# Attention denominators spread by a VectorE shuffle, per-slot restacking and a new order of work in two six-layer transformer stacks

## The reference

```python
def _L2_xcond_ref(x, noise_emb, context, src_mask, ctx_mask, ...):      # _L3_xcond_ref is the same
    NL, D, H, DFF = (6, 128, 16, 512); HD = D // H
    def _adaln(x, emb, w, b):
        g, be = jnp.split(emb[:, 0, :] @ w.T + b, 2, axis=-1)
        return _ln(x) * (1.0 + g[:, None, :]) + be[:, None, :]
    def _attn(q, k, v, mask):
        scores = jnp.einsum('bqhd,bkhd->bhqk', q, k) / np.float32(np.sqrt(HD))
        scores = jnp.where(mask[:, None, None, :], -jnp.inf, scores)
        return jnp.einsum('bhqk,bkhd->bqhd', jax.nn.softmax(scores, axis=-1), v)
    for i in range(NL):
        xn = _adaln(x, noise_emb, n1_w[i], n1_b[i])
        q, k, v = jnp.split(xn @ qkv_w[i].T, 3, axis=-1)
        x = x + _attn(_rope(q), _rope(k), v, src_mask) @ so_w[i].T
        xn = _adaln(x, noise_emb, n2_w[i], n2_b[i])
        q, k, v = _rope(xn @ cq_w[i].T), _rope(context @ ck_w[i].T), context @ cv_w[i].T
        x = x + _attn(q, k, v, ctx_mask) @ co_w[i].T
        xn = _adaln(x, noise_emb, n3_w[i], n3_b[i])
        x = x + (gelu(xn @ f1_w[i].T + f1_b[i]) @ f2_w[i].T + f2_b[i])
    return x
```

## Time and profile before

| | us |
|---|---|
| median of 3 runs (lowest, highest) | 3263.07 (3258.29, 3272.04) |
| the profiled execution | 3272.75 |
| its span, first to last instruction | 3269.9 |
| first stack / second stack, from the page's chain | about 680 to 1888 / about 1950 to 3157 |
| TensorE busy, share of the span | 2898.2 (89%) |
| VectorE busy | 2097.7 (64%) |
| ScalarE busy | 1911.0 (58%) |
| GpSimd busy | 829.6 (25%) |
| mean granted TensorE clock | 0.959 of full |

### The profile page before, as it was taken

One profiled execution on the slowest core, in us unless ns is written; L12 is line 12 of the kernel. 1 busy time (PEld: TensorE's weight loads), 2 busy tenths in 40 slices (PEclk: granted clock), 3 DMA queues, 4 the chain that ended last, 5 costly groups with the idle time before them and its releaser, 6 DMA issues.

```text
span 3269.9 us, 44850 instructions
## 1 busy us (share of the span) xinstructions
PE 2898.2 (89%) x15711; PEld 1035.8 (32%) x15711; DVE 2097.7 (64%) x3628; ACT 1911.0 (58%) x2677; POOL 829.6 (25%) x1327
## 2 busy tenths in 40 slices
PE   7999999869989898998989866989989898998978
PEld 2474433322322223232222221232323223232236
DVE  4317777548486774957668377668485775948634
ACT  5533443427667584766758534758566684766742
POOL 0003556612312222222222102212222222222211
PEclk9999999979999998999999877999999999999999
DMA  1101000001111111111111101011111111111130
GB/s 46 59 1 26 1 1 1 11 20 38 41 30 36 42 33 41 32 38 43 39 30 40 34 7 42 23 38 39 49 27 38 44 28 41 39 42 35 36 130 7
DMA packets 125513, 110.10 MB, mean 34 GB/s; under 512 B 49982, under 2 KB 116076, under 8 KB 125292
## 3 DMA queue, kind: packets, MB, share of 16 engines
q1 hardware_dynamic: 114924, 97.80, 10.1%
q10 hardware_dynamic: 10368, 9.44, 1.0%
HBM read 41.96 MB, written 0.52 MB: 13 GB/s over the span
## 4 chain that ended last, share of the span: by engine, by line
PE 68%; DVE 17%; ACT 5%; issue 4%; POOL 2%; SPq 1%; ACTq 1%; DMA 1%; DVEq 0%; POOLq 0%
PE ps L524 12%; DVE arena L812 7%; PE ps L469 7%; PE ps L498 3%; PE ps L640 3%; PE ps L655 3%; PE ps L597 3%; PE ps L541 3%; PE ps L583 2%; PE ps L1521 2%; PE ps L1509 2%; PE ps L532 2%; PE ps L572 2%; PE ps L553 2%; PE ps L1467 2%
## 5 line engine op out<-in xcount | busy, mean ns | idle before, releaser
L680 ACT ACTIVATE arena<-ps 128x1024 f32<-128x1024 f32 x960 | 934.7, 1022 | 246.6 <-PE ps L498 236.5
L812 DVE TENSOR_REDUCE arena<-ps 128x1 f32<-128x512 f32 x1536 | 965.0, 684 | 125.3 <-PE ps L469 115.7
L524 PE MATMUL ps<-arena 128*32 128x512 f32 x3840 | 504.1, 606 | 2.2 <-ACT arena L699 1.1
L469 PE MATMUL ps<-arena 49*128 49x512 bf16 x1536 | 313.3, 404 | 151.7 <-DVE arena L812 107.3
L814 DVE TENSOR_REDUCE arena<-ps 128x3 f32<-128x462 f32 (+1 forms) x576 | 305.5, 580 | 134.1 <-PE ps L476 113.6
L498 PE MATMUL ps<-arena 52*128 52x512 bf16 x1920 | 343.2, 385 | 29.8 <-DMA arena<-arena 9.4
L902 POOL TENSOR_TENSOR arena<-arena,zeros 128x16 bf16<-128x16 f32 x192 | 42.3, 220 | 1088.8 <-DVE arena L812 715.7
L469 PEld LDWEIGHTS ps<-arena 49*128 49x128 bf16 x1536 | 75.0, 93 | 548.5 <-DVE arena L812 473.7
L912 POOL TENSOR_TENSOR arena<-arena 128x512 f32<-128x512 f32 x96 | 122.1, 1272 | 387.5 <-ACT arena L712 384.3
L1579 ACT ACTIVATE arena<-ps 128x1024 f32<-128x1024 f32 x96 | 98.2, 1023 | 172.0 <-DVE ps L1664 112.8
L362 PE MATMUL ps<-consts 128*128 128x512 f32 x336 | 162.0, 607 | 23.7 <-DVE arena L2101 23.7
(11 more groups left out here) (391 smaller groups left out, 4338.3 us busy)
## 6 DMA issues: line engine op xcount, KB each, us to landing
arena<-arena SPq DMA_DIRECT2D x720, 64.0 KB
arena<-we_dram SPq DMA_DIRECT2D x24, 578.5 KB, 7.6
arena<-arena ACTq DMA_DIRECT2D x144, 64.0 KB
w<-weights_dram SPq DMA_DIRECT2D x26, 320.0 KB, 3.3
w<-weights_dram SPq DMA_DIRECT2D x13, 512.0 KB, 4.0
arena<-arena SPq DMA_DIRECT2D x384, 6.0 KB
arena<-arena SPq DMA_DIRECT2D x288, 19.2 KB
w<-weights_dram SPq DMA_DIRECT2D x39, 128.0 KB, 2.2
```

The source lines that it names most:

```text
L469: pe.matmul(s_bank(slot + r), qst[b][rows, idx, P * qt:P * (qt + 1)], kst[b][rows, idx, :], start=True, stop=True).then_inc(s_full, 1)
L524: mm = pe.matmul(bank(7)[32 * j:32 * j + 32, :], v, prob[:, slot, j, :], start=(g % 2 == 0 and kt == 0), stop=(a == 0 and g % 2 == 1 and k ...
L680: act.activation(prob[:, chunk_no(b, a, g, kt) % NPROB, 2 * p:2 * p + 2, :], e_bank(slot).rearrange("p (j n) -> p j n", j=2), ACT.Exp, sca ...
L812: op = ve.tensor_reduce(nmax[:, g % 2, r, n:n + 1], s_bank(slot + r), AX.X, ALU.max, negate=True)
```

## The change

Four things change in the two stacks.

1. `sel` moves from TensorE to VectorE: a `stream_shuffle` copies row 8 to the first 16 and row 24 to the last 16 rows of each 32 partitions of `osb`, into `rlog`. ScalarE takes the logarithm in place from there. The `selector2` matrix and its setup go, and `sel` no longer takes a double bank of ring "e".
2. A self-attention `score` no longer waits for two free banks before its first matmul: each of its two matmuls waits for its own bank. On VectorE and ScalarE some pairs of waits stand in the other order.
3. Restacking is ordered by slot, not by part: 24 `st` places of one slot each for q and k of a batch's self attention and so on, 42 `st` items per layer in place of 21. Ten slots per layer (20 DMAs) are issued by ScalarE, before two parts with three slots each (12 DMAs).
4. `PLACES` is new, with 392 items, and `FILL` has 16 fillers per layer, in place of 9: six of them now stand ahead of scores of batch 0's self attention, and `sel`'s eight matmuls per layer are gone.

```diff
-PER_LAYER = 371
+PER_LAYER = 392
 PLACES = {
-    ('sel', 0): [[141, 144], [285, 287]],
+    ('sel', 0): [[117, 159], [293, 302]],
...
-        def restack(eng, b, u, part):
-            for slot in slots_of(u, part):
-                for r in range(2):
...
+        def restack(eng, b, u, slot):
+            part = part_in(u, slot)
+            for r in range(2):
+                rows = slice(64 * r + slot, 64 * r + ROW_MASK, PARTS)
...
-        ACT_STACKS = (("st", 0, 1, 0), ("st", 1, 2, 0))
-        FILL = {("out", 0, 1): 3, ("out", 1, 1): 2, ("f1", 0, 0): 1, ("score", 1, 1, 0, 0): 2, ("center", 0, 2): 1}
+        ACT_STACKS = (("st", 0, 0, 2), ("st", 0, 1, 0), ("st", 0, 2, 5), ("st", 1, 0, 0), ("st", 1, 0, 4),
+                      ("st", 1, 1, 1), ("st", 1, 1, 2), ("st", 1, 1, 5), ("st", 1, 2, 1), ("st", 1, 2, 3))
+        FILL = {('center', 0, 0): 1, ('center', 0, 2): 1, ('out', 0, 1): 1, ('out', 1, 1): 3, ('proj', 1, 2):
+                1, ('score', 0, 0, 0, 2): 1, ('score', 0, 0, 0, 5): 1, ('score', 0, 0, 0, 6): 1, ('score', 0,
+                0, 0, 7): 1, ('score', 0, 0, 1, 0): 1, ('score', 0, 0, 1, 4): 1, ('score', 1, 1, 0, 0): 2,
+                ('var', 0, 2): 1}
             def score(it):
-                pe.wait_ge(s_free, z.room("s", it, 2))
                 if a == 0:
                     for r in range(2):
                         rows = slice(64 * r, 64 * r + K_SCORE)
+                        pe.wait_ge(s_free, z.room("s", it, 1) if r == 0 else floor0(at - 1))
                         pe.matmul(...)
                     return
+                pe.wait_ge(s_free, z.room("s", it, 2))
...
-            def sel(it):                                              # TensorE
-                pe.wait_ge(v_free, z.after("evac", ("evac", b, a, e), it))
-                pe.wait_ge(e_free, z.room("e", it, 1))
-                pe.matmul(e_bank(slot)[:, 0:S], selector2[:, :], osb[:, e, :], start=True, stop=True)\
-                  .then_inc(e_full, 1)
...
             def sel(it):                                              # ScalarE
-                act.wait_ge(e_full, at + 1)
-                act.wait_ge(den_inv, z.ahead("inv", it))
-                act.activation(rlog, e_bank(slot)[:, 0:S], ACT.Ln).then_inc(e_free, 1)
+                act.wait_ge(den_spread, z.after("sel", it))
+                act.activation(rlog, rlog, ACT.Ln).then_inc(den_log, 1)
             def stack(it):                                            # ScalarE
                 if it in ACT_STACKS:
-                    act.wait_ge(part_hi, z.after("hi", ("hi", b, u), it))
-                    restack(act, b, u, part)
+                    act.wait_ge((part_hi, part_mid, part_lo)[part_in(u, slot)], z.after("hi", ("hi", b, u), it))
+                    restack(act, b, u, slot)
...
+            def sel(it):                                              # VectorE
+                ve.wait_ge(v_free, z.after("evac", ("evac", b, a, e), it))
+                ve.wait_ge(den_inv, z.ahead("inv", it))
+                ve.stream_shuffle(rlog, osb[:, e, :], [HD] * 16 + [16 + HD] * 16).then_inc(den_spread, 1)
```

More of the change, by code:

```diff
@@ L139 @@
+    ('st', 1): [[63, 78, 83, 80, 64, 81], [91, 73, 70, 88, 87, 85], [308, 311, 317, 309, 310, 312]],
+    ('ktail',): 185,
+    ('vals',): [4, 119, -1],
+    ('f1',): [[320, 323], [424, 426]],
+    ('f2',): [327, 428],
+    ('gain',): [-77, 95, 227],
+    ('biasf',): 167,
+    ('load',): {'cout': 560, 'cross': 306, 'ffn': 584, 'n0': 46, 'n1': 284, 'n2': 392, 'self': 174, 'sout':
+        341},
 }
@@ L442, in build @@
[L442 to L446 removed]
+        def restack(eng, b, u, slot):
+            part = part_in(u, slot)
+            for r in range(2):
+                rows = slice(64 * r + slot, 64 * r + ROW_MASK, PARTS)
+                if u == 3:
+                    for bb in range(B):
+                        eng.dma_start(kstc[bb][rows, :, 0:CTX],
+                                      parts_c[r::2, part, bb * CTX:(bb + 1) * CTX]).then_inc(stacked_c, 16)
+                else:
+                    eng.dma_start((kst if u == 1 else qst)[b][rows, :, :], unit_parts(b, u)[r::2, part, :])\
+                       .then_inc(stacked(b, u), 16)
@@ L492, in exp @@
                 slot, at = z.use("e", it)
+                if it in FILL:
+                    pe.wait_ge(e_free, z.room("e", it, 1))
+                    fill(it, e_bank(slot)[:, 0:S])
                 if p == 0 and kt == 0:
@@ L588, in proj @@
                 slot, at = z.use("s", it)
+                if it in FILL:
+                    pe.wait_ge(s_free, z.room("s", it, 1))
+                    fill(it, s_bank(slot))
                 if u == 3:
@@ L963, in stack @@
             def stack(it):
-                _, b, u, part = it
+                _, b, u, slot = it
                 if it not in ACT_STACKS:
-                    sp.wait_ge((part_hi, part_mid, part_lo)[part], z.after("hi", ("hi", b, u), it))
-                    restack(sp, b, u, part)
+                    sp.wait_ge((part_hi, part_mid, part_lo)[part_in(u, slot)], z.after("hi", ("hi", b, u), it))
+                    restack(sp, b, u, slot)
             def load(it):
```

150 lines of the change are left out of this document (62 added, 88 removed), and 3 rows, old and new, of the table PLACES.

## The result

| | before | after |
|---|---|---|
| median of the runs on one chip (lowest, highest) | 3267.56 (3258.29, 3273.62), 4 runs | 3372.35 (3342.46, 3382.82), 4 runs |
| the profiled execution | 3272.75 | 3369.27 |
| its span | 3269.9 | 3367.4 |
| mean granted clock | 0.959 | 0.943 |
| mean period of batch 0's `f2`, ten layers | 193.97 | 201.06 |

The changed kernel is 3.0% slower: ratio 1.0295, 95% interval 1.0250 to 1.0339. The forecast was 3216 us with a range up to 3285; it failed in sign. Of the 97.5 us between the spans 71.0 lie in the ten periods, 12.2 in the piece between the stacks (1895.49 to 2209.54, 314.1 us against 301.9), 11.0 ahead of the first `f2` and 3.3 behind the last.

A forecast was written before the change was run, and what follows sets the result against it. Per layer, VectorE, then TensorE, then batch 0's serial path were taken as the bound; terms summed to -4.4 us, ten times -44, with first layers -47 in all, from 3263.07 to 3216 us, range 3150 to 3285.

The forecast's parts named there:

- the six fillers: Among batch 0's first scores: no cost at 2.4 GHz, and clock loss cut by 2.3 us per layer, bounds 0 and -3.5.
- the forecast's own: The main forecast's narrower range for the whole kernel, 3190 to 3245 us, with chance 0.49.
- Rival C: Fillers at batch 0's first scores run at half clock: +6.2 us, clock gain gone, slower at 3301 us; chance 0.15.
- The clock: At a layer's start: mean layer loses 3.5 us to clock falls; fillers there win back two thirds, -2.3 us.
- Serial path: Batch 0's path from output projection to restacking: shorter by 2.4 us at its start and 0.4 us at its end.
- Start: Before batch 0's norm: 0.9 us from selector pair replaced by filler, 1.4 us from fewer ScalarE DMAs; together -2.4 us.
- End: From batch 0's q projection to next layer's first score: 1.9 us saved, 1.5 us added, sum -0.4 us.
- The +1.5 us: At the layer's end: SyncE issues 20 restacking DMAs instead of 18, at 0.74 us each, costing +1.5 us.
- the VectorE-bound stretch: First score of batch 0 to first selector product, 71.8 us: VectorE, busy 64.6 us with score maxima, sets the pace.
- Selector products: Four single products on the chain in the TensorE-bound stretch go: -2.1 us per layer, between 0 and -4.2.
- the shuffles: On VectorE, 0.6 us each, three of eight where it is short of time: +1.8 us per layer, bounds +1.5 and +4.4.
- ScalarE's DMAs for batch 1's self attention: Ten DMAs moved from SyncE into the stretch VectorE bounds, mostly covered: +1.0 us per layer, bounds 0 and +7.2.

The follow-up runs named there:

- e2: Changed kernel, with each self-attention score filler waiting only for the one bank it writes, not both: 3256.01 us, ratio 0.9969.
- e1: Changed kernel without its six fillers ahead of batch 0's first self-attention scores: 3285.86 us, ratio 1.0062.
- e4: Kernel before, plus six fillers ahead of the same scores, each waiting for both banks: 3323.53 us, ratio 1.0181.
- e8: Changed kernel with score fillers waiting for one bank, and the selector product back on TensorE in place of the shuffle: 3348.19 us, ratio 1.0253.
- e3: Changed kernel's shuffle and split score waits, with the places, ScalarE DMAs and fillers of the kernel before: 3365.56 us, ratio 1.0308.
- e10: Changed kernel with one-bank filler waits, three of six score fillers, and two more ahead of the first self score pair: 3292.56 us, ratio 1.0067.

## Why the prediction was wrong

**The step that failed** is the one on the six fillers: "At full clock a score pair and a filler hold TensorE 0.39 + 0.9 = 1.3 us, the two maxima VectorE 2 x 0.63 = 1.26 us (965.0/1536): nothing at 2.4 GHz." It adds up occupation and takes for granted that filler and maxima run side by side. They don't: the filler waits for both banks. Measured: 2.23 us in place of 1.3, and 5.0 us a layer at full clock where I had 0 (after against e2). The clock went the other way as well: what the mean layer loses to it rose from 3.5 to 6.4 us, where I had it fall by 2.3. The wait stood in the code; I read what the filler costs and not what it waits for. With that one wait changed (e2) the kernel comes out at 3256 us, 10 us under before, in the range but not in the forecast's own.

**Rival C** named the right place and sign, and reached 3301 us. Its condition, a fallen clock, was not needed: 4.2 of the 7.1 us by which the mean layer is longer are there at 2.4 GHz. Its size was too small, since it too let the filler run beside the maxima: 2.3 us from pair to pair at half clock, where 3.39 was measured.

**The clock.** The prediction that fillers at these scores hold the clock was right, and in e2 larger than I took: against e1 3.7 us a layer. After's late fillers leave TensorE idle for 0.78 us ahead of each, and nine of ten layers fell below 1.00. But e4 has the same late fillers, and five of its ten layers stay at 1.00: why the clock fell so often in after is open.

**Serial path.** Start: ScalarE's DMAs ahead of the square take 1.7 us less (predicted 1.4). End: 1.8 us less (predicted 0.4), because 20 DMAs took SyncE no longer than 18. The +1.5 us came from a wrong reading of the earlier trace rows: "0.74 us each" spread the 1.3 us of waiting for GpSimd over the 18. The two DMAs more do cost 1.3 us, and the order by slot took the wait away, a gain that I didn't see. In e2 the stretch from batch 1's self-attention `out` to batch 0's next `f2` shrank from 35.3 to 28.7 us, also because TensorE has 7.0 us less work in it; here before, then e2:

```profile
1217.23:1252.54 35.31, 33.06 (x159) 12.30 (x157) 12.05 (x24) 21.33 (x29) 7.61 (x13) 1.00 0.12 35
```

```profile
2298.33:2327.07 28.74, 26.07 (x116) 9.30 (x114) 13.81 (x23) 14.96 (x23) 6.82 (x9) 1.00 0.13 40
```

**Where that gain went.** Before's stretch from first score to `out` of batch 0:

```profile
1096.12:1173.37 77.25, 67.76 (x393) 19.77 (x394) 69.64 (x114) 54.37 (x75) 16.86 (x33) 1.00 0.10 29
```

In e2 it is 83.50 us, 6.2 longer, and VectorE is busy 75.80, 6.2 more (idle 7.6 and 7.7 us): VectorE sets its length, as the prediction read. The new order puts 105 maxima into it where there were 99 (65.9 us for 62.0) and two shuffles (1.5 us). So the gain behind is given back in front. The two stretches that are left change by -1.2 us (`f2` to first score, 34.1 to 32.9) and +1.3 us (`out` to `out`, 43.9 to 45.2), and a full-clock layer stays at 190.3 against 190.5. "The prediction is wrong at its root if the VectorE-bound stretch grows by more than 5 us": taken to batch 0's `out`, since after has no selector product to end it, it grew by 11.2, 6.2 of it work that the new order put there and 5.0 the fillers' series. My terms were summed stretch by stretch as if the borders stayed where they were.

**Selector products and shuffles.** The products were taken as -2.1 us (0 to -4.2), the shuffles as +1.8. e8 prices the products at 7.8 us a layer in the new places, e3 the shuffle at 8 us in the old ones. With each in its own order the layers are equally long (190.3 and 190.5 us). A single number for "replace A by B" does not exist apart from the list that it stands in. The shuffle's own duration, 0.727 us where I took 0.6, is a small error.

**Not tried alone:** ScalarE's DMAs for batch 1's self attention (taken as +1.0 us), restacking by slot, and the swapped waits. What each of them is worth is not shown.

## What to carry to other kernels

Before adding work "in a gap", write down what its own wait is and draw the chain through it: a filler that waits for more buffers than it writes turns from cover into a link of the series. Add up occupation only for instructions that may overlap, and check that the gap is empty in this order, not in another. And count what an order moves into each bounded stretch before summing the gains of the others.

## What the runs showed of the hardware

With early fillers among the first pairs of a layer the granted clock stayed at 1.00 in seven of ten layers (e2); without them it fell in all ten (e1), though in the layer compared TensorE's busy time in the 8 us ahead was alike, 5.9 and 5.5 us. 1.9 us of fillers right ahead of the scores, beside three among them, did not do the same: no layer of e10 is at 1.00. A shuffle over 128x512 f32 in SBUF is 727 ns, preceded by a mask load of 14 ns. The issue of a 64 KB restacking DMA takes SyncE 0.66 to 0.67 us where nothing holds it up (20 in 13.20 us, 12 in 8.07 us); ScalarE's rows have 0.66 us in a row of four and 0.72 in a row of six.
